# Gathers without a bound on the index: five stages of a graph network on one core

## The chip, the cores and the metric

The kernel runs on one core of a Trainium2 chip. The metric is the device time of one execution in microseconds (us). The kernel before took 9419.78 us, the median of three runs (9418.16 to 9432.5).

A core has five engines with queues of their own: TensorE (PE; its weight loads are PEld), VectorE (DVE), ScalarE (ACT), GpSimd (POOL) and SyncE (SP, which only issues transfers here). Sixteen DMA engines move the data. Gathers and scatters by a list of row numbers are issued on GpSimd.

## The reference

There are 100,000 nodes with 64 features each and 50,000 edges (`src`, `dst`), sorted by `dst`. Four layers follow one another, and each ends in a layer norm of the input plus the layer's output:

```python
def _tag_conv(x, row, col, norm, W, b):            # layer 0, twice, K = 5
    out = x @ W[0]
    h = x
    for k in range(1, K + 1):
        msg = h[row] * norm[:, None]
        h = jax.ops.segment_sum(msg, col, num_segments=N_NODES)
        out = out + h @ W[k]
    return out + b
# layer 1: mean over neighbours, then attention over edges and the node itself
agg = segment_sum(x[src], dst) / max(count, 1)
h = agg @ W_sl + b_sl + x @ W_sr
xl, xr = h @ Wg_l + bg_l, h @ Wg_r + bg_r           # 4 heads
logit = einsum('ehd,hd->eh', leaky_relu(xl[s2] + xr[d2], 0.2), att)
out = segment_sum(softmax(logit) * xl[s2], d2).mean(heads) + b_gat
# layer 2: relu(mean of (x @ W)[src] + x @ root + bias)
# layer 3: attention with logits a_src[src] + a_dst[dst], then a dense layer
```

Every `[src]` in it is a gather of rows, once for each of the 50,000 edges.

## The kernel before

The edges stand in 128 partitions of 391 columns each (`T = 391`, column T is padding), so one column is 128 edges, one in each partition. One gather fetches the source rows of one column: 128 rows of 64 to 68 floats from a table in device memory into a tile, by a list of 128 row numbers that stands in on-chip memory, one in each partition. Eight columns make a group (`K8 = 8`), 49 groups a stage (`NG`), and one stage has 391 gathers. The gathers of a stage go into a ring of six groups (`RING = 6`): before group g is gathered, GpSimd waits until group g - 6 has been consumed.

What happens in the order of time:

- The rows of x for all `dst` nodes are gathered (table `in_x_dram`), and beside it lie the dense layers of all nodes, computed as if no edge came in (the other nodes have rows of their own behind). They go on in slices beside most later stages of layer 0.
- First hop, kind "placed": rows of `x_with_place` (66 floats) by `src_index`. Every index is a node number below 100,000.
- Three more hops and the top stage gather by `place_of_source`: the row of the edge at which the source node's sum stands. A source without an edge into it has no such row; its index is set far outside of the table, the gather skips it by the bound, and what was in the tile before is multiplied by a weight of zero. Five more stages of the second convolution do the same with the tables y and u (nine stages by `place_of_source` in all, with 391 gathers each).
- Mean stage of layer 1 (table x1), by `row_of_source` (`comb`): a table that holds the 100,000 nodes followed by the rows of the edge places, 150,176 rows, so each index lies in it. VectorE sums the gathered columns (line 861), then TensorE, ScalarE and VectorE run 15 to 16 dependent steps for each group in three lanes.
- Pair stage of layer 1 (`logits2`, table `h_sage`), by `row_of_source`: TensorE turns the pairs of rows (line 2144) and computes the edge logits.
- The softmax terms and the attention sums of layer 1, without gathers apart from one.
- Mean stage of layer 2 (table x2), by `row_of_source`.
- Source rows of layer 3 (`logits3`, table x3), by `row_of_source`: VectorE adds the logits (line 2368), and SyncE writes the features back.
- Softmax terms and attention sums of layer 3, with a scatter of 392 columns into the output (line 2700), its index bounded as well.

All gathers go through one helper, `gather` (line 810, its instruction has line 812 in the profile), which gives each gather a bound and asks that an index over it be skipped in silence. `stage_gpsimd` (line 816) issues the gathers of the hops, of the up stages and of the two mean stages; the pair stage and the source rows have loops of their own. The order of the work is written out by hand: each engine has its own program, and waits are on semaphores.

Of the kernel before, what the change touches and what calls it, by code (L numbers as in the profile page):

```python
# [12 lines left out]
N = 100000  # L13
E = 50000
D = 64
# [8 lines left out]
RP = P * C  # L24
BLOCK = P * K8
DB = 98
CB = N
# [3 lines left out]
RING = 6  # L31
# [77 lines left out]
def bass_gnn_resnorm(nc, x, src, dst, edge_weight, edge_weight1, W0, b0, W1, b1, W_sl, b_sl, W_sr, Wg_l, bg_l,  # L109
# [21 lines left out]
    x66_rows = x66.rearrange("(n a) b -> n (a b)", a=XW // 2)  # L131
    xc = dram("xc", (RP, D))
    hop = [xc] + [dram(f"hop{k}", (RP, D)) for k in range(1, HOPS)]
# [4 lines left out]
    hh, x3 = (dram(n, (CB + RP, XL)) for n in ("h_sage", "x3"))  # L138
# [10 lines left out]
    srci = sb(stack, "src_index", [P, C], I32)  # L149
    comb = sb(stack, "row_of_source", [P, C], I32)  # L150
# [617 lines left out]
    norm, carried_b = PS[4][:, 0:C], PS[4][:, C:C + D]  # L768
# [40 lines left out]

    def gather(e, tab, index, into, top):  # L810

        return e.indirect_dma_start(out=into, out_offset=None, in_=tab,  # L812
                                    in_offset=bass.IndirectOffsetOnAxis(ap=index, axis=0), bounds_check=top,
                                    oob_is_err=False)

    def stage_gpsimd(e, st):
        top = e.to_reg(st.top)
        for g in range(NG):
            if g >= RING and st.weight is None:
                e.wait_ge(*st.summed((g - RING + 1) * K8))  # L820
            elif g >= RING:
                e.wait_ge(*st.weighed(g - RING + 1))
            for k in range(tiles(g)):
                t = g * K8 + k
                into = ring[g % RING][:, k, 0:XW if st.placed else D]
                gather(e, st.table, st.index[:, t:t + 1], into, top).then_inc(st.gathered[g % RING].handle, 16)
        if st.by_row:
            e.wait_ge(*st.headed(1))
            for i in range(3):
                e.wait_ge(*st.stored[i](16 * len(range(i, NG - 2, 3))))  # L830
            gather(e, st.into, early_row[:, 0:1], early_sum[0][:, :], RP - 1).then_inc(st.found_head.handle, 16)
# [216 lines left out]
    def main():  # L1048
        with ExitStack() as ctx:
# [72 lines left out]
            xs_out = [sem(f"x_out{i}", 16 * len(range(i, DB, 3))) for i in range(3)]  # L1122
            combined, lned = sem("combined", 4), sem("logarithm", NG)
            diag = sb(ctx, "first_dst", [P, P])
            hops = [Stage(x66_rows, N - 1, srci, norm, "placed", into=hop[1])]
            for k in range(2, HOPS):
                hops.append(Stage(hop[k - 1], RP - 1, found, norm, "hop", into=hop[k]))
            top = Stage(hop[HOPS - 1], RP - 1, found, norm, "top")
# [843 lines left out]
    def mean_stage(kind, tab, into, parts, own_part=None):  # L1972
        with ExitStack() as ctx:
            stage_buffers(ctx)
            st = Stage(tab, CB + RP - 1, comb, None, "mean")
            names = ("raw1", "raw2", "xT", "aT") + (("z0", "z1", "z2", "z3", "lin") if kind == "h" else ("a", "tmp"))
            lanes = [Work(ctx, f"lane{l}", MEAN_STEPS[kind], len(range(l, NG, MEAN_LANES)), [two], names, (1,), wide=(0,),
                          **(dict(full=OWN_ROUNDS, short=MEAN_SHORT) if kind == "h" else {}))
                     for l, two in enumerate(((PS[0], PS[1]), (PS[2], PS[3]), (PS[5], PS[6])))]
            for l, W in enumerate(lanes):  # L1980
                W.place = l

                def keep(r, _, l=l):
                    at = (MEAN_LANES * r + l) * K8
                    return parts[:, at:at + K8, :]

                def keep_own(r, _, l=l):
                    at = (MEAN_LANES * r + l) * K8
                    return own_part[:, at:at + K8, :]
                W.keep, W.keep_own = keep, keep_own  # L1990
            with nc.Block() as block:
                @block.gpsimd
                def _(e):
                    stage_gpsimd(e, st)

                @block.sync
                def _(e):
                    means_sync(e, lanes, kind, tab, into)

                @block.tensor  # L2000
                def _(e):
                    means_tensor(e, st, lanes, kind)

                @block.scalar
                def _(e):
                    mean_steps(lambda W: mean_scalar(e, W, kind), lanes).end()

                @block.vector
                def _(e):
                    means_vector(e, st, lanes, kind)  # L2010
# [67 lines left out]
    def logits2(parts, own_part, lg):  # L2078
        ORDER = list(range(NG))[::-1]
        PW = D + XL  # L2080
# [12 lines left out]
        got = [sem(f"row_gathered{i}", 16 * n) for i, n in enumerate([sum(tiles(g) for g in ORDER[i::RING]) for i in range(RING)])]  # L2093
# [6 lines left out]
        with ExitStack() as ctx:  # L2100
# [135 lines left out]
            with nc.Block() as block:  # L2236
# [28 lines left out]
                @block.gpsimd  # L2265
                def _(e):
                    e.wait_ge(*last_moved(1))
                    last_row = e.to_reg(CB + RP - 1)
                    for i in range(NG):
                        g = ORDER[i]  # L2270
                        if i >= RING:
                            e.wait_ge(*put[i % RING](16 * (i // RING)))
                            e.wait_ge(*taken(i - RING + 1))
                            e.wait_ge(*at(i - RING, 1))
                        for k in range(tiles(g)):
                            t = g * K8 + k
                            gather(e, hh, comb[:, t:t + 1], pair[i % RING][:, k, D:PW], last_row).then_inc(got[i % RING].handle, 16)

                @block.tensor
                def _(e):  # L2280
# [39 lines left out]
    def logits3(parts, lg):  # L2320
        fv, ft = sem("fill_vector", len(FILL)), sem("fill_tensor", 1)
        got = [sem(f"row_gathered{i}", 16 * n) for i, n in enumerate(in_slots(RING, tiles))]
        put = [sem(f"features_stored{i}", 16 * n) for i, n in enumerate(in_slots(RING, lambda g: 1))]
        met, done = sem("rows_met", NG), sem("logits_done", NG)
        with ExitStack() as ctx:
            rows_ = [sb(ctx, f"source_row{i}", [P, K8, XL]) for i in range(RING)]
            own = sb(ctx, "own_parts", [P, H2, C])
            fill = sb(ctx, "parts_of_node", [P, H2, C])
            last = sb(ctx, "parts_after", [P, H2])
            z = [sb(ctx, f"edge_logits{i}", [P, HEADS, K8]) for i in range(2)]  # L2330

            def got_all(g):
                return got[g % RING](16 * (K8 * (g // RING) + tiles(g)))

            with nc.Block() as block:
                @block.sync
                def _(e):
                    for g in range(NG):
                        e.wait_ge(*got_all(g))
                        e.dma_start(columns(hs_t, g)[:, 0:tiles(g), :], rows_[g % RING][:, 0:tiles(g), 0:D]  # L2340
                                    ).then_inc(put[g % RING].handle, 16)
                    for i in range(RING):
                        e.wait_ge(*put[i](16 * in_slots(RING, lambda g: 1)[i]))

                @block.gpsimd
                def _(e):
                    last_row = e.to_reg(CB + RP - 1)
                    for g in range(NG):
                        if g >= RING:
                            e.wait_ge(*put[g % RING](16 * (g // RING)))  # L2350
                            e.wait_ge(*met(g - RING + 1))
                        for k in range(tiles(g)):
                            t = g * K8 + k
                            gather(e, x3, comb[:, t:t + 1], rows_[g % RING][:, k, :], last_row).then_inc(got[g % RING].handle, 16)

                @block.tensor
                def _(e):
                    fill_tensor(e, fv, ft, own, PS[0])

                @block.vector  # L2360
                def _(e):
                    fill_vector(e, fv, ft, parts, own, fill, last, PS[0], lg)
                    for g in range(NG):
                        c, k = slice(g * K8, g * K8 + tiles(g)), tiles(g)
                        e.wait_ge(*got_all(g))
                        if g >= 2:
                            e.wait_ge(*done(g - 1))
                        e.tensor_tensor(z[g % 2][:, :, 0:k], rows_[g % RING][:, 0:k, D:XL].rearrange("p k h -> p h k"),
                                        own[:, 0:HEADS, c], ALU.add).then_inc(met.handle, 1)
                        e.wait_ge(*met(g + 1))  # L2370
                        e.scalar_tensor_tensor(lg[:, 0:HEADS, c], z[g % 2][:, :, 0:k], 0.2, z[g % 2][:, :, 0:k], ALU.mult,
                                               ALU.max).then_inc(done.handle, 1)
# [446 lines left out]
```

## Time and profile before

| what | value |
|---|---|
| median of the runs | 9419.78 us |
| span of the profiled execution | 9425.4 us |
| GpSimd busy | 6467.0 us, 69% of the span |
| TensorE busy | 5731.8 us, 61% |
| VectorE busy | 5330.6 us, 57% |
| ScalarE busy | 3226.1 us, 34% |
| gathers and scatters on GpSimd | 6264 instructions |
| bytes by GpSimd's DMA queue (q0) | 130.29 MB |

The profile is of one execution. Its span, from the first instruction to the last, is 5.6 us (0.06%) above the median of the runs, with next to nothing around it, so a difference worked out in the trace can be taken off either. Busy time of an engine is a sum over stages with different limits; a stage is judged by the engine that never waits in it.

### The profile page before, as it was taken

What the parts mean: (1) busy time and instruction counts of PE and PEld (TensorE: products, weight loads), DVE (VectorE), ACT (ScalarE), POOL (GpSimd) and SP (SyncE); (2) the same over time, 40 slices, a digit from 0 to 9 for tenths busy, and PEclk for the clock granted to TensorE, in tenths of its full rate; (3) what the DMA queues carried; (4) which work ended last, traced back from release to release, by engine and by line L of the source; (5) the groups of instructions that cost most, each with busy time, mean ns of one, the idle gap of its engine ahead of it and who ended that gap; (6) DMA issues with size and microseconds to landing.
All of it is one profiled execution on the core that took longest, in us unless ns stands there. A gap on an engine that the chain in (4) does not pass through costs nothing. (4 is left out here: it accounts for less than half of the span.)

```text
span 9425.4 us, 77459 instructions
## 1 busy us (share of the span) xinstructions
PE 5731.8 (61%) x19953; PEld 3098.8 (33%) x19953; DVE 5330.6 (57%) x14589; ACT 3226.1 (34%) x5537; POOL 6467.0 (69%) x6274
## 2 busy tenths in 40 slices
PE   6656565665669865564646200598997976610397
PEld 5623232333335422232323100243334644300264
DVE  4235454554546566666656588544458965510596
ACT  0034343443423333343424101243445753300153
POOL 7777777777777577777777777775770017767477
PEclk7578787887879977787778655799998988855698
DMA  6764332332369733232323222222334532222353
GB/s 164 127 141 120 99 104 86 103 103 86 103 173 261 224 94 99 89 100 84 104 85 99 80 76 81 66 72 70 80 76 139 188 125 75 73 48 52 91 178 119
DMA packets 1086302, 1021.92 MB, mean 108 GB/s; under 512 B 653551, under 2 KB 709245, under 8 KB 1073313
## 3 DMA queue, kind: packets, MB, share of 16 engines
q1 hardware_dynamic: 847422, 884.62, 30.3%
q0 software_dynamic: 200480, 130.29, 7.8%
q10 hardware_dynamic: 37955, 2.05, 0.4%
q8 instruction: 160, 2.62, 0.1%
q14 instruction: 285, 2.33, 0.1%
HBM read 494.44 MB, written 599.31 MB: 116 GB/s over the span
## 5 line engine op out<-in xcount | busy, mean ns | idle before, releaser
L812 POOL DMA_INDIRECT gathered<-u,place_of_source x1564 | 1641.3, 1049 | 512.9 <-issue 475.3
L812 POOL DMA_INDIRECT gathered<-hop,place_of_source x1564 | 1608.0, 1028 | 508.5 <-issue 475.3
L847 DVE TENSOR_TENSOR weighted<-gathered,bank 128x512 f32<-128x512 f32 (+1 forms) x490 | 335.7, 685 | 1408.6 <-DMA gathered<-hop,place_of_source 688.0
L861 DVE SCALAR_TENSOR_TENSOR sums<-sums,same_as_before,weighted 128x64 f32<-128x64 f32 x3510 | 987.2, 281 | 96.3 <-DVE weighted L847 40.8
L812 POOL DMA_INDIRECT gathered<-x,row_of_source x782 | 806.5, 1031 | 298.3 <-issue 234.6
L874 DVE SCALAR_TENSOR_TENSOR first_node_sum<-sums,ends_first,first_node_sum 128x64 f32<-128x64 f32 x2786 | 782.2, 281 | 7.1 <-DVE sums L861 5.9
L531 PE MATMUL bank<-dense_tmp,mean 128*128 128x512 f32 x980 | 527.1, 654 | 77.7 <-ACT dense_tmp L540 76.2
L2700 POOL DMA_INDIRECT out_dram<-lane_out,node_to_write x392 | 396.0, 1010 | 215.6 <-issue 116.1
L812 POOL DMA_INDIRECT gathered<-y,place_of_source x391 | 408.1, 1044 | 187.5 <-issue 118.8
L835 PE MATMUL bank<-sums,goes_on_into 128*128 128x64 f32 x22 | 7.6, 448 | 857.7 <-DVE sums L861 857.7
L812 POOL DMA_INDIRECT pair<-h_sage,row_of_source x391 | 406.6, 1040 | 171.7 <-issue 117.3
L531 PE MATMUL bank<-dense_a,center 128*128 128x512 f32 x588 | 416.7, 823 | 163.4 <-DVE dense_a L555 109.8
L812 POOL DMA_INDIRECT source_row<-x,row_of_source x391 | 397.7, 1017 | 153.9 <-issue 118.8
L812 POOL DMA_INDIRECT gathered<-x_with_place,src_index x391 | 400.3, 1024 | 138.1 <-issue 137.8
L812 POOL DMA_INDIRECT gathered<-in_x_dram,dst_index x392 | 394.2, 1006 | 135.5 <-issue 117.9
L531 PE MATMUL bank<-dense_yT,bd_l 128*128 128x512 f32 x196 | 184.5, 1041 | 473.6 <-DVE dense_out L516 473.4
L812 POOL DMA_INDIRECT first_sum<-head_sums,row_of_first_end x2 | 2.0, 1025 | 616.1 <-DMA head_sums<-head_sums 615.8
L2742 DVE SCALAR_TENSOR_TENSOR head_sums<-head_sums,same_as_before 128x256 f32<-128x256 f32 x780 | 380.1, 487 | 24.5
L2563 PE MATMUL bank<-ident,heads 128*128 128x128 f32 x1568 | 361.8, 278 | 41.0 <-issue 18.5
L861 DVE SCALAR_TENSOR_TENSOR sums<-sums,same_as_before,gathered 128x64 f32<-128x64 f32 x780 | 218.2, 280 | 269.1 <-DMA gathered<-x,row_of_source 269.0
L2564 PE MATMUL bank<-ident,head_sums 128*128 128x128 f32 x1568 | 357.6, 275 | 0.0
L542 ACT ACTIVATE dense_tmp<-bank,eps_col 128x512 f32<-128x512 f32 x490 | 332.3, 678 | 52.2 <-PE bank L531 51.6
(533 smaller groups left out, 14427.4 us busy)
## 6 DMA issues: line engine op xcount, KB each, us to landing
head_sums<-head_sums SPq DMA_DIRECT2D x98, 1024.0 KB, 4.7
y<-conv_out SPq DMA_DIRECT2D x294, 256.0 KB
conv_out<-y SPq DMA_DIRECT2D x245, 256.0 KB, 3.2
hop<-sums SPq DMA_DIRECT2D x196, 256.0 KB, 2.0
turned<-rows_turned SPq DMA_DIRECT2D x196, 256.0 KB, 2.7
cat<-turned SPq DMA_DIRECT2D x196, 256.0 KB
u<-conv_out SPq DMA_DIRECT2D x196, 256.0 KB, 2.0
lane_raw<-x SPq DMA_DIRECT2D x196, 256.0 KB
```

What stands on the lines that cost most here:

```text
L531: m = e.matmul(W.bank[l][b][:, :], w, W.b(v, l), start=i == 0, stop=i == len(pairs) - 1)
L542: m = e.activation(W.b(o, l), src_ap, func, bias=v[:, 0:1], scale=scale)
L812: return e.indirect_dma_start(out=into, out_offset=None, in_=tab, in_offset=bass.IndirectOffsetOnAxis(ap=index, axis=0), bounds_check=top, ...
L835: e.matmul(carried_b, link[:], s[:, K8 - 2, :], start=True, stop=True).then_inc(st.carried.handle, 1)
L847: e.tensor_tensor(weighted[g % 2][:, 0:n, :], st.rows_of(g), over(st.weight[:, cols], D), ALU.mult).then_inc(st.weighed.handle, 1)
L861: e.scalar_tensor_tensor(s[:, k, :], b, go[:, t:t + 1], m[:, k, :], ALU.mult, ALU.add).then_inc(st.summed.handle, 1)
L874: e.scalar_tensor_tensor(h, row_, flast[:, t:t + 1], h, ALU.mult, ALU.add).then_inc(st.headed.handle, 1)
L2563: e.matmul(to, o[:, at_], ident[:], start=True, stop=False, is_transpose=True)
L2564: m = e.matmul(to, s[:, at_], ident[:], start=False, stop=True, is_transpose=True)
L2700: e.indirect_dma_start(out=out, out_offset=bass.IndirectOffsetOnAxis(ap=scat[:, t:t + 1], axis=0), in_=W.out[0][0][:, k * D:(k + 1) * D], ...
L2742: e.scalar_tensor_tensor(s[:, k, :], b, go[:, t:t + 1], s[:, k, :], ALU.mult, ALU.add).then_inc(summed.handle, 1)
```

## The change

A gather may now be called with no bound (`top` is None). Five stages do so: the first hop, the mean stages of layers 1 and 2, the pair stage and the source rows, with 391 gathers each. The other gathers and the scatter keep the bound and the silent skip. In the call without a bound, `oob_is_err=False` is left out as well. No instruction changes its place on any engine; five register moves on GpSimd go, one for each of the five stages, since no register is loaded with the bound.

```diff
     def gather(e, tab, index, into, top):
 
-        return e.indirect_dma_start(out=into, out_offset=None, in_=tab,
-                                    in_offset=bass.IndirectOffsetOnAxis(ap=index, axis=0), bounds_check=top,
-                                    oob_is_err=False)
+        at = bass.IndirectOffsetOnAxis(ap=index, axis=0)
+        if top is None:
+            return e.indirect_dma_start(out=into, out_offset=None, in_=tab, in_offset=at)
+        return e.indirect_dma_start(out=into, out_offset=None, in_=tab, in_offset=at, bounds_check=top, oob_is_err=False)
 
     def stage_gpsimd(e, st):
-        top = e.to_reg(st.top)
+        top = None if st.top is None else e.to_reg(st.top)
...
-            hops = [Stage(x66_rows, N - 1, srci, norm, "placed", into=hop[1])]
+            hops = [Stage(x66_rows, None, srci, norm, "placed", into=hop[1])]
...
-            st = Stage(tab, CB + RP - 1, comb, None, "mean")
+            st = Stage(tab, None, comb, None, "mean")
...
-                    last_row = e.to_reg(CB + RP - 1)
...
-                            gather(e, hh, comb[:, t:t + 1], pair[i % RING][:, k, D:PW], last_row).then_inc(got[i % RING].handle, 16)
+                            gather(e, hh, comb[:, t:t + 1], pair[i % RING][:, k, D:PW], None).then_inc(got[i % RING].handle, 16)
...
-                    last_row = e.to_reg(CB + RP - 1)
...
-                            gather(e, x3, comb[:, t:t + 1], rows_[g % RING][:, k, :], last_row).then_inc(got[g % RING].handle, 16)
+                            gather(e, x3, comb[:, t:t + 1], rows_[g % RING][:, k, :], None).then_inc(got[g % RING].handle, 16)
```

## Rows read from the trace of the kernel before

**Rows 1.** The profile's page, part 1: busy us of each engine.
```profile
PE 5731.8 (61%) x19953; PEld 3098.8 (33%) x19953; DVE 5330.6 (57%) x14589; ACT 3226.1 (34%) x5537; POOL 6467.0 (69%) x6274
```

**Rows 2.** Groups on GpSimd: count, busy us, mean ns of one, idle before.
```profile
L812 POOL DMA_INDIRECT gathered<-x,row_of_source x782 | 806.5, 1031 | 298.3 <-issue 234.6 <-POOLq L2636 37.8 <-POOLq L1534 18.4
...
L812 POOL DMA_INDIRECT source_row<-x,row_of_source x391 | 397.7, 1017 | 153.9 <-issue 118.8 <-ACTq L2335 35.0
...
L1540 POOL IOTA sums<- 128x496 int32 x1 | 0.5, 540 | 0.0
L1538 POOL IOTA conv_out<- 128x392 int32 x1 | 0.5, 453 | 6.5 <-DVE same_as_next L1789 6.5
...
L288 POOL TENSOR_SCALAR_AFFINE_SELECT ident<-ident 128x128 f32<-128x128 f32 x1 | 0.3, 292 | 4.1 <-DVE eps_col L334 4.1
```

**Rows 3.** GpSimd in order of time, source rows: start us, duration us, idle before.
```profile
8400.04 0.99 POOL L812 DMA_INDIRECT source_row<-x,row_of_source  x1 [0.30 <-issue]
8401.34 0.99 POOL L812 DMA_INDIRECT source_row<-x,row_of_source  x1 [0.30 <-issue]
```

**Rows 4.** Busy us by stage: first hop, mean 1, pair, mean 2, source rows.
```profile
562.00:1081.20 519.20, 321.25 (x1013) 168.01 (x1011) 272.00 (x741) 224.76 (x383) 400.31 (x391) 0.79 0.39 113
...
5971.20:6488.30 517.10, 491.06 (x1652) 202.85 (x1652) 212.50 (x944) 201.00 (x331) 393.71 (x391) 0.96 0.27 70
6541.10:7066.50 525.40, 471.25 (x1498) 173.80 (x1498) 266.60 (x1007) 229.23 (x375) 406.55 (x391) 0.96 0.38 78
7721.10:8252.70 531.60, 346.59 (x1102) 203.24 (x1102) 279.41 (x1082) 168.04 (x276) 412.74 (x391) 0.79 0.29 72
8287.70:8804.20 516.50, 0.60 (x2) 0.50 (x2) 41.44 (x119) 0.00 (x0) 397.69 (x391) 0.50 0.26 51
```

**Rows 5.** Line 812 in the source rows: duration min/median/max ns, and who waited.
```profile
L812 POOL DMA_INDIRECT source_row<-x,row_of_source x391: 992/997/3142, 8287.7 to 8803.2; - x196
...
  DVE edge_logits L2368: 474.8, 48
```

**Rows 6.** Waits of 562 to 1090, first hop: us in total, times, longest.
```profile
DVE bank L843 <- DMA gathered<-x_with_place,src_index: 179.8, 46, 7.7
```

**Rows 7.** Waits of 7721 to 8290, mean stage of layer 2.
```profile
DVE sums L861 <- DMA gathered<-x,row_of_source: 241.2, 48, 6.8
```

**Rows 8.** Waits of 6541 to 7080, pair stage.
```profile
PEld bank L2144 <- DMA pair<-h_sage,row_of_source: 48.2, 21, 4.4
...
PE bank L2144 <- DMA pair<-h_sage,row_of_source: 29.0, 14, 3.4
```

**Rows 9.** Mean stage of layer 1, busy us within 100 us, as in group 4.
```profile
6300.00:6400.00 100.00, 100.00 (x339) 40.35 (x337) 43.33 (x191) 40.65 (x68) 76.55 (x78) 1.00 0.28 74
```

**Rows 10.** Line 861 in the mean stage of layer 1: duration ns, first and last.
```profile
L861 DVE SCALAR_TENSOR_TENSOR sums<-sums,same_as_before,gathered x390: 270/279/327, 5983.1 to 6520.2; 128x64 f32<-128x64 f32 x195
```

**Rows 11.** Line 812 in the same stage: duration ns, first and last start us.
```profile
L812 POOL DMA_INDIRECT gathered<-x,row_of_source x391: 992/997/1399, 5971.2 to 6487.3; - x196
...
  DVE sums L861: 7.5, 10
```

**Rows 12.** GpSimd in order of time, mean stage of layer 1, ring full.
```profile
6430.02 0.99 POOL L812 DMA_INDIRECT gathered<-x,row_of_source  x1 [0.30 <-issue]
6432.00 1.39 POOL L812 DMA_INDIRECT gathered<-x,row_of_source  x1 [0.99 <-DVE sums L861]
```

**Rows 13.** Line 812 in a hop by place of source: duration min/median/max ns.
```profile
L812 POOL DMA_INDIRECT gathered<-hop,place_of_source x391: 991/997/1608, 1090.3 to 1610.5; - x196
L812 POOLq MOVE  x1: 29/29/29, 1599.1 to 1599.1; - x1
```

**Rows 14.** GpSimd's DMA queue, 1100 to 1600, that hop: packets, MB, share.
```profile
q0 software_dynamic: 11984, 4.45, 5.6%
```

**Rows 15.** GpSimd's DMA queue, 8300 to 8800, source rows.
```profile
q0 software_dynamic: 12223, 13.32, 15.9%
```

**Rows 16.** The scatter into the output, line 2700: duration min/median/max ns.
```profile
L2700 POOL DMA_INDIRECT out_dram<-lane_out,node_to_write x392: 980/982/1238, 8899.0 to 9416.2; - x196
```

## The prediction, made before the result was known

> **What bounds the kernel now.** I read the busy times first, then the groups on GpSimd, then each stage for itself. No engine is busy all the time [rows 1], but GpSimd's 69% understates it: between two gathers of a stage it stands for 0.30 us with nothing to wait for [rows 3], time that the page calls issue. The typical gather takes 0.997 us [rows 5], so one column costs 1.30 us, and 391 of them about 509 us. The five stages that the change touches last 517 to 532 us from the first gather to the end of the last [rows 4]. Four of them are therefore one unbroken train of gathers.
>
> Who waits for whom says the same. In the first hop VectorE stood 179.8 us, 46 times, for the gathers of a group [rows 6], in the mean stage of layer 2 241.2 us [rows 7], and in the source rows 474.8 us, where TensorE and ScalarE do nothing at all [rows 4, 5]. In the pair stage TensorE is busy 471 of 525 us, and its queue still stood 48.2 us for gathered rows at the weight loads and 29.0 us at the matmuls [rows 8]: GpSimd sets the pace, with little in hand.
>
> The mean stage of layer 1 is the odd one. TensorE is busy for 100.00 of 100 us at a granted clock of 1.00, the upper of its two levels, 2.4 GHz [rows 9]. The gathers start from 5971.2 to 6487.3, but the sums that consume them from 5983.1 to 6520.2 [rows 10, 11]: 12 us behind at the start, 33 us at the end. From 6432.0 on the ring of six groups is full, and GpSimd waits for VectorE's sums [rows 12], ten waits of 7.5 us in all [rows 11]. That stage ends when TensorE is through, not when the gathers are.
>
> **The change part by part.** Nothing is added and nothing moves. It removes the bound from 5 x 391 = 1955 gathers, and five register moves of 29 ns on GpSimd [rows 13], 0.15 us in all, which I leave out. The count of gathers, their sizes, the ring and all waits stay. The whole effect is then one number, the ns that a gather takes less (or more) without its bound, times the gathers that stand on the path.
>
> The path: the first hop, the pair stage, the mean stage of layer 2 and the source rows count in full, 4 x 391 = 1564 gathers. The mean stage of layer 1 counts nothing as long as the saving is small: a faster GpSimd only fills the ring earlier and then waits longer for the sums. The work that covers its 391 gathers is TensorE's, 491 us of the 517 [rows 4]. Were TensorE no cover, a saving of s ns would be worth 0.391 s us more.
>
> What one bound costs the trace of before doesn't show, since every gather in it has one. The nearest rows bound it:
>
> - What the check decides costs no time. In a hop by place of source GpSimd's queue moved 4.45 MB in 11,984 packets within 500 us, in the source rows 13.32 MB in 12,223 [rows 14, 15]. At 1.30 us a gather that is 32 packets each, while the bytes fall from 272 for each row to about 92 (256 without a skip): most rows of the hop are skipped, and each leaves its entry behind. Yet both have the same typical duration, 997 ns, and the same fastest, 991 and 992 [rows 5, 13]. So there is no branch for a skipped row that would make the gather shorter; if the check costs time, it is the same for every index.
> - Upper end: a compare and select over 128 indices one after another. IOTA takes 453 ns for 392 columns and 540 for 496 [rows 2], so 0.84 ns a column after a start of about 125. An AFFINE_SELECT, which compares and selects, over 128 columns takes 292 ns, 167 above that start [rows 2].
> - Lower end: the indices stand one in each partition, so one column of such a compare might do for all: 167 / 128 = 1.3 ns.
> - The nearest row is that of another form of the same instruction. The scatter has as many indices, also bounded, on the other side of the transfer, and takes 982 ns instead of 997 [rows 16, 5], 15 ns less. That is how much these forms differ, and it bounds the other sign as well: without the bound a gather might also take 15 ns more.
>
> I take 15 ns, the one difference measured between two forms of this instruction, and nearer to the lower end than to the upper. The sum: 1564 x 15 = 23.5 us. Against the profiled span it is 9425.4 - 23.5 = 9401.9; that span lies 5.6 us above the median, so the time forecast is 9419.8 - 23.5 = 9396.3.
>
> A rule speaks against the change. The rows show 32 packets for each gather with and without skipped rows, and one typical duration [rows 5, 13 to 15]. The Trainium skill, page "DMA: Bandwidth & Descriptors", section "SWDGE vs HWDGE vs iDMA", says that a transfer issued on GpSimd has its descriptors computed by software, one pair for each operation, and written into rings. If that writing were the whole of the 997 ns, the change would take nothing off, since the number of entries is set by the 128 indices: the time would be 9419.8. The trace agrees that the entries stay; no row shows what part of the 997 ns they are.
>
> **The rivals.**
>
> - The bound costs nothing: it is one operation among many for all indices, or the instruction compares with some bound in any case, and the lower end of 1.3 ns holds. For it: the duration that doesn't move with the share of skipped rows. Against it: skipped rows are given another size, so something is selected for each row, and forms of the instruction do differ by 15 ns. 1564 x 1.3 = 2 us, 9418.
> - The bound costs much, 40 ns or more, as in a loop over the indices. For it: 997 ns for 128 indices is 7.8 ns for each, the length of a loop rather than of one operation for all. Against it: nothing but the missing evidence. Then the pair stage stops giving when TensorE no longer waits for rows, at most 48.2 us, which is reached at 123 ns a gather; and the mean stage of layer 1 still gives nothing. At 80 ns: 4 x 391 x 80 = 125 us, if TensorE's waits in the pair stage all go, 9295. At the upper end, 167 ns: 3 x 391 x 167 + 48.2 = 244 us, 9176.
> - Slower. The new call drops `oob_is_err=False` together with the bound, so by its argument an index out of the table is now an error and no longer skipped. If this form tests each index and reports instead of selecting a size, a gather takes longer, and by the 15 ns between two forms it is 1564 x 15 = 23.5 us, 9443. It decides from 12 ns a gather (0.2% of the time). For it: the argument in the diff. Against it: without a bound there is nothing to test against except the table's own size, which the call doesn't name. The mean stage of layer 1 would hide it too.
> - TensorE is no cover in the mean stage of layer 1. That adds 0.391 x 15 = 5.9 us of gain, 9390; the full ring speaks against it.
>
> **How the numbers follow.** A difference under 0.2%, 19 us, can't be told from no change by a measurement of this kernel; over 1564 gathers that is 12 ns each. The forecast, a saving of 6 to 40 ns, has 39% (its own range is 9357 to 9410), 8 of them below 12 ns; the last rival shares these. No cost, under 6 ns in either direction, 30%. Much, 40 ns and more, 17%. Longer by over 6 ns, 14%, 2 of them within 12 ns. So faster is 31 + 17 = 48%, no change 8 + 30 + 2 = 40%, slower 12%. The range reaches up to 13 ns longer, 9440, and down to 100 ns saved: 3 x 391 x 100 + 39 = 156 us, 9264, rounded to 9265. What is left out below is the rest of the way to 9176, some 8%, above some 7%.
>
> **What would show it.** Line by line in the profile after: the gathers without a bound by their minimum and median (997 before), the gathers that keep it and the scatter, which must stay at 997 and 982; the idle 0.30 us before each gather, where the cost could stand instead of in the duration; the five stages' lengths, of which the mean stage of layer 1 should keep its end while its ring is full earlier and the waits for the sums grow from 7.5 us (by some 5.9); and the queue's 32 packets a gather. I am wrong if the unbounded gathers differ by nothing (then 9418), if they take longer, or if the stages don't shorten by 391 times what one gather saves.

## The result and the profile after

The changed kernel takes 9338.08 us, the median of four runs (9333.71 to 9342.84), against 9422.83 us for the kernel before beside it: 84.8 us less, a ratio of 0.9911 with a 95% interval of 0.9899 to 0.9923. The forecast was 9396 us within 9265 to 9440.

The groups on GpSimd tell most of it (count, busy us, mean ns of one, idle before). Line 814 is now the gather without a bound, line 815 the one that keeps it, and line 2699 the scatter.

```profile
L815 POOL DMA_INDIRECT gathered<-hop,place_of_source x1564 | 1606.6, 1027 | 506.9 <-issue 475.4 <-DMA hop<-sums 31.5
L814 POOL DMA_INDIRECT gathered<-x,row_of_source x782 | 765.2, 978 | 305.9 <-issue 232.3 <-POOLq L2635 38.0 <-DVE sums L862 18.0
...
L814 POOL DMA_INDIRECT source_row<-x,row_of_source x391 | 377.9, 967 | 153.5 <-issue 118.8 <-ACTq L2335 34.7
```

The means fall by 50 ns in the source rows (from 1017 in [rows 2]) and by 53 ns in the two mean stages together (from 1031). The 53 there is an average of two unlike numbers: by the busy times of [rows 4] and of the table below, the mean falls by 26 ns in layer 1 (1007 to 981) and by 80 in layer 2 (1056 to 976). Minimum, median and maximum of one instruction show the step without the disturbed ones; here are line 814 in the source rows with its waiter, line 815 in the hop of [rows 13], and the scatter:

```profile
L814 POOL DMA_INDIRECT source_row<-x,row_of_source x391: 940/944/3146, 8213.6 to 8709.4; - x196
...
  DVE edge_logits L2367: 454.7, 48
```
```profile
L815 POOL DMA_INDIRECT gathered<-hop,place_of_source x391: 992/997/1600, 1070.8 to 1589.1; - x196
```
```profile
L2699 POOL DMA_INDIRECT out_dram<-lane_out,node_to_write x392: 982/982/1251, 8805.5 to 9322.8; - x196
```

Without its bound a gather takes 944 ns where it took 997 [rows 5]; the idle before it is the same (118.8 us over 390 gathers, 0.305 us each), and the forms that keep the bound stay at 997 and 982. So s, the one unknown of the prediction, is 53 ns.

Busy us by stage (columns as in [rows 4]: length, then PE, PEld, DVE, ACT and POOL, granted clock, DMA share, GB/s):

```profile
562.10:1061.70 499.60, 313.12 (x1014) 163.81 (x1012) 272.49 (x741) 224.81 (x383) 380.73 (x391) 0.82 0.40 117
5943.90:6458.80 514.90, 489.82 (x1648) 201.94 (x1649) 211.41 (x944) 200.41 (x330) 383.55 (x391) 0.96 0.26 71
6511.50:7023.70 512.20, 468.04 (x1498) 171.87 (x1498) 266.56 (x1007) 228.80 (x375) 393.28 (x391) 0.97 0.38 80
7678.40:8178.90 500.50, 335.34 (x1098) 192.32 (x1099) 279.45 (x1082) 166.82 (x276) 381.59 (x391) 0.81 0.29 76
8213.60:8710.30 496.70, 0.60 (x2) 0.50 (x2) 41.69 (x119) 0.00 (x0) 377.86 (x391) 0.50 0.26 53
```

From the first gather of a stage to the first one of the next (for the source rows: to the first scatter), the first hop lasts 508.7 us instead of 528.3, the mean stage of layer 1 567.6 instead of 569.9, the pair stage with what follows it 1166.9 instead of 1180.0, the mean stage of layer 2 535.2 instead of 566.6, and the source rows with the softmax terms 591.9 instead of 611.3. That is 19.6, 2.3, 13.1, 31.4 and 19.4 us, 85.8 together. The spans of the two profiled executions differ by 93.4 us (9425.4 and 9332.0); the other 7.6 us lie in stages that the change doesn't touch. (All these are differences of one profiled execution each.)

The mean stage of layer 1 does what the prediction said. Line 862, the sums, with its waiters, and TensorE within 50 us:

```profile
L862 DVE SCALAR_TENSOR_TENSOR sums<-sums,same_as_before,gathered x390: 266/277/325, 5955.3 to 6491.2; 128x64 f32<-128x64 f32 x195
...
  POOL gathered L814: 18.0, 18
```
```profile
6300.00:6350.00 50.00, 50.00 (x170) 20.27 (x168) 21.08 (x95) 20.72 (x34) 38.00 (x40) 1.00 0.26 70
```

The sums run over 535.9 us instead of 537.1 [rows 10], though the gathers are 53 ns shorter; GpSimd waits for them 18 times, 18.0 us, instead of 7.5 [rows 11]. Its gathers there are busy for 383.6 us instead of 393.7, so the 10 us that they gave up came back as waiting.

### The profile page after: what moved, and what is told of

Read it like the earlier page. It is cut to its first block and busy times, and to the rows that moved or that the text cites. A ratio compares the mean times of both kernels' runs of the same rounds, so it can differ in the third digit from the quotient of the medians.

```text
span 9332.0 us, 77454 instructions
## 1 busy us (share of the span) xinstructions
PE 5706.7 (61%) x19953; PEld 3078.5 (33%) x19953; DVE 5329.1 (57%) x14589; ACT 3223.6 (35%) x5537; POOL 6368.2 (68%) x6274
## 5 line engine op out<-in xcount | busy, mean ns | idle before, releaser
L814 POOL DMA_INDIRECT gathered<-x,row_of_source x782 | 765.2, 978 | 305.9 <-issue 232.3
L2699 POOL DMA_INDIRECT out_dram<-lane_out,node_to_write x392 | 395.8, 1010 | 216.2 <-issue 116.4
L815 POOL DMA_INDIRECT gathered<-y,place_of_source x391 | 405.8, 1038 | 187.0 <-issue 118.8
L814 POOL DMA_INDIRECT pair<-h_sage,row_of_source x391 | 393.3, 1006 | 171.6 <-issue 113.7
L815 POOL DMA_INDIRECT gathered<-in_x_dram,dst_index x392 | 394.4, 1006 | 135.7 <-issue 118.2
L814 POOL DMA_INDIRECT source_row<-x,row_of_source x391 | 377.9, 967 | 153.5 <-issue 118.8
L814 POOL DMA_INDIRECT gathered<-x_with_place,src_index x391 | 380.7, 974 | 137.8 <-issue 137.8
```

What stands on the lines that cost most here:

```text
L2699: e.indirect_dma_start(out=out, out_offset=bass.IndirectOffsetOnAxis(ap=scat[:, t:t + 1], axis=0), in_=W.out[0][0][:, k * D:(k + 1) * D], ...
```

## The experiments

**The changed kernel again, and the bound put back stage by stage.** Four kernels on one chip. One is the changed kernel again, the mark for the others; in the other three one stage has its bound again: the mean stage of layer 1, the pair stage, and the mean stage of layer 2.

```diff
-            st = Stage(tab, None, comb, None, "mean")
+            st = Stage(tab, CB + RP - 1 if kind == "h" else None, comb, None, "mean")
```
```diff
...
-                            gather(e, hh, comb[:, t:t + 1], pair[i % RING][:, k, D:PW], None).then_inc(got[i % RING].handle, 16)
+                            gather(e, hh, comb[:, t:t + 1], pair[i % RING][:, k, D:PW], last_row).then_inc(got[i % RING].handle, 16)
...
```
```diff
-            st = Stage(tab, None, comb, None, "mean")
+            st = Stage(tab, CB + RP - 1 if kind == "x3" else None, comb, None, "mean")
```

The mark, without any bound put back:

> The changed kernel again, as the mark for the three others of this call. If the gain is the sum of its stages as the two traces have it (first hop 19.5, mean stage of layer 1 2.3, pair stage 13.1, mean stage of layer 2 31.4, source rows 19.4 us, together 85.7), it is 80 to 92 us below the kernel before on this chip too, and its profile has unbounded gathers of 944 ns median. If the 31.4 us of the mean stage of layer 2 were the luck of one profiled execution, its mean of a gather there (976 ns) lies 20 ns or more away from that.

It took 9337.26 us, ratio 0.9913 [0.9899, 0.9926], so 84.3 us below the kernel before here. But in its mean stage of layer 2 a gather takes 1004 ns on average, not 976, as the groups within the stage show, first of the changed kernel's first profile, then of this one:

```profile
L814 POOL DMA_INDIRECT gathered<-x,row_of_source x391 | 381.6, 976 | 156.9 <-issue 118.9 <-POOLq L2635 38.0
```
```profile
L814 POOL DMA_INDIRECT gathered<-x,row_of_source x391 | 392.6, 1004 | 154.2 <-issue 118.8 <-POOLq L2635 35.4
```

That is 28 ns away, so part of the 31.4 us there was the luck of one execution. The bound in the mean stage of layer 1:

> The changed kernel with the bound put back in the mean stage of layer 1 alone. Theory (TensorE ends that stage, the bound there is hidden): 0 to 5 us above the changed kernel; its gathers are 997 ns again, the stage from its first gather to the first gather of the pair stage is 570 us instead of 567.6. Rival (gathers count there as everywhere): 391 x 53 ns = 20.7 us above.

9335.79 us, ratio 0.9909 [0.9893, 0.9924]: 1.5 us below the mark, no difference. GpSimd's group in that stage, with its wait for the sums, of this kernel:

```profile
L815 POOL DMA_INDIRECT gathered<-x,row_of_source x391 | 394.2, 1008 | 140.7 <-issue 113.6 <-POOLq L1535 17.7 <-DVE sums L862 9.4
```

The 391 gathers are 53 ns longer at the median (997 again) and 27 ns at the mean (1008 against 981), which puts 10.6 us back on GpSimd; its wait for the sums shrinks to 9.4 us, and nothing ends later. That these gathers are not on the path is shown, not only argued; that TensorE is what covers them rests on its busy share. The pair stage:

> The changed kernel with the bound put back in the pair stage alone. Theory (the faster gathers lose 8 of their 20.7 us to work of VectorE that they now meet): 11 to 16 us above the changed kernel, mean of a gather about 1040 ns against 1006. Rival (each gather counts in full): 20.7 us above. Second rival (TensorE takes over): under 8 us, and TensorE waits no longer for gathered rows in the changed kernel.

9350.92 us, ratio 0.9931 [0.9917, 0.9945]: 13.7 us above the mark. First this kernel's group, then that of the changed kernel's first profile:

```profile
L815 POOL DMA_INDIRECT pair<-h_sage,row_of_source x391 | 405.7, 1038 | 171.8 <-issue 117.0 <-DVE pair L2297 53.0 <-ACT quad_z L2183 1.5
```
```profile
L814 POOL DMA_INDIRECT pair<-h_sage,row_of_source x391 | 393.3, 1006 | 171.6 <-issue 113.7 <-DVE pair L2296 52.7 <-ACT quad_z L2183 2.1
```

32 ns for each of 391 gathers are 12.5 us: the time follows the mean of a gather, and the median's 53 ns don't arrive in full. TensorE hasn't taken over, since it still waits for gathered rows, 37.9 us at the weight loads (48.2 before, [rows 8]). The mean stage of layer 2:

> The changed kernel with the bound put back in the mean stage of layer 2 alone. Theory (20.7 us by the bound, and some 11 us because the sixth gather of a group no longer meets VectorE's multiply of 128x512): 27 to 35 us above the changed kernel, mean of a gather about 1056 ns against 976. Rival (the 11 us are chance): 18 to 23 us above, mean of a gather under 1035 ns.

9363.77 us, ratio 0.994 [0.9927, 0.9954]: 26.5 us above the mark, between what the two expected. Its gathers there:

```profile
L815 POOL DMA_INDIRECT gathered<-x,row_of_source x391 | 411.5, 1053 | 157.5 <-issue 118.8 <-POOLq L2635 38.7
```

1053 ns, where the profile of before has 1056, while the four profiles so far without the bound there (the changed kernel's two and those of the two kernels just told of) show 976, 1004, 989 and 992, 990 on average. 63 x 391 ns are 24.6 us: 20.7 by the bound and some 4 because, on the average of the four, fewer gathers are held up, so 7 of the 31.4 us were chance. The columns differ, too: of the 23 us that the gathers of this stage exceed their median by in the profile of before, 19 fall on the sixth of each group of eight, the one that VectorE's multiply of 128x512 mostly overlaps. What that overlap does is read further down.

**Which part of the bound costs.** One kernel gathers the source rows, where the other engines are nearly idle, in all forms side by side:

```diff
+                            if k in (0, 3, 6):
+                                e.indirect_dma_start(out=r[:, k, :], out_offset=None, in_=x3, in_offset=at(t)).then_inc(s_, 16)
+                            elif k in (1, 4, 7):
+                                e.indirect_dma_start(out=r[:, k, :], out_offset=None, in_=x3, in_offset=at(t), bounds_check=last_row, oob_is_err=False).then_inc(s_, 16)
+                            else:
+                                e.indirect_dma_start(out=r[:, k, :], out_offset=None, in_=x3, in_offset=at(t), bounds_check=last_row, oob_is_err=True).then_inc(s_, 16)
+                            if k == 3:
+                                e.indirect_dma_start(out=h[0:N2, 0, :], out_offset=None, in_=x3, in_offset=at(t, N2)).then_inc(s_, 16)
+                            if k == 4:
+                                e.indirect_dma_start(out=h[0:N2, 1, :], out_offset=None, in_=x3, in_offset=at(t, N2), bounds_check=last_row, oob_is_err=False).then_inc(s_, 16)
...
```

> The changed kernel, whose source-row stage (VectorE and TensorE nearly idle) gathers its columns in three forms in turn: without a bound, with the bound and the silent skip, with the bound and an index over it as an error; and for two columns of each group 64 of the 128 rows once more into a spare tile, without and with the bound. Theory (the test against the bound costs): 944, 997 and 997 ns. Rival (the silent skip costs): 944, 997 and 944 ns. A cost for each index halves with 64 rows: 26 ns between the two halves; a cost for each instruction stays 53 ns. If the whole gather is a loop over its indices, 64 rows take some 500 ns; if it is fixed, over 800.

Minimum, median and maximum ns, in the order of the diff: no bound (line 2359), silent skip (2361), error (2363), 64 rows without (2365) and with a bound (2367):

```profile
L2359 POOL DMA_INDIRECT source_row<-x,row_of_source x147: 953/957/3083, 8220.7 to 8855.5; - x147
...
L2361 POOL DMA_INDIRECT source_row<-x,row_of_source x146: 992/997/2640, 8222.7 to 8851.6; - x146
...
L2363 POOL DMA_INDIRECT source_row<-x,row_of_source x98: 1012/1024/1767, 8225.6 to 8854.2; - x98
...
L2365 POOL DMA_INDIRECT half_row<-x,row_of_source x49: 905/909/921, 8230.9 to 8850.4; - x49
...
L2367 POOL DMA_INDIRECT half_row<-x,row_of_source x49: 947/951/1244, 8233.8 to 8852.9; - x49
```

(Its one run, 9480.47 us, holds 98 gathers more than the changed kernel.) The silent skip isn't what costs: with an error instead of the skip the gather is longest. It is the bound in either form; whether comparing with it or fetching it costs, no run separates. Its price doesn't halve with the rows: it is 42 ns with 64 rows (951 - 909), and 40 with 128 in this kernel (997 - 957), 53 in stages of one form. So of the two rivals on its shape a price for each instruction is nearer. And 64 rows take 909 ns, only 35 to 48 less than 128 (944 or 957), so the gather is almost wholly a cost of the instruction. Its packets don't halve either. The changed kernel's queue over the whole span, then this kernel's with its 98 gathers of 64 rows:

```profile
q0 software_dynamic: 200480, 130.29, 7.4%
```
```profile
q0 software_dynamic: 203616, 132.00, 7.1%
```

The 3136 packets more are 32 for each of the 98, as for 128 rows.

One thing is confounded here: in this mixture a gather without a bound takes 957 instead of 944. It isn't simply the form of the gather before it, since in the kernel with two forms in turn (below) those that follow one of their like at the border of two groups take 957, too, at the median of 24 in either mean stage. The cause stays open. A kernel with one form alone settles the order:

```diff
...
-                                    oob_is_err=False)
+                                    oob_is_err=err)
...
-                gather(e, st.table, st.index[:, t:t + 1], into, top).then_inc(st.gathered[g % RING].handle, 16)
+                gather(e, st.table, st.index[:, t:t + 1], into, top, st.kind in ("placed", "mean")).then_inc(st.gathered[g % RING].handle, 16)
...
```

> The kernel before, whose gathers in the five stages keep the bound but name an index over it an error (no index is). Theory (the test costs): the time of the kernel before within 8 us, 997 ns. Rival (the silent skip costs): the changed kernel's time, some 84 us below, 944 ns. Third (the error form costs extra): above the kernel before.

```profile
L812 POOL DMA_INDIRECT source_row<-x,row_of_source x391: 1006/1010/3141, 8291.9 to 8812.6; - x196
```

9439.06 us, ratio 1.0025 [1.0015, 1.0035]: slower than the kernel before, by some 23 us on this chip (9416.35 there). The third expectation held. 1564 x 13 ns are 20.3 us.

**Are gathers without a bound held up more?** The excess over the median in the pair stage grew with the change (1040 - 997 = 43 ns before; 1006 - 945 = 61 in the changed kernel's first profile, 50 in its second), so both forms were set side by side there and in the mean stages:

```diff
...
-                            gather(e, hh, comb[:, t:t + 1], pair[i % RING][:, k, D:PW], None).then_inc(got[i % RING].handle, 16)
+                            gather(e, hh, comb[:, t:t + 1], pair[i % RING][:, k, D:PW], row_ if (k + i) % 2 else None).then_inc(got[i % RING].handle, 16)
```

> The changed kernel, whose gathers in the two mean stages and in the pair stage have the bound or not in turn, column by column, so both forms meet the same work of VectorE. The excess of a gather's mean over its median in the pair stage was 43 ns with the bound and 50 to 62 without. If the form without a bound is held up more by VectorE, its excess in the pair stage is again 10 ns or more above the other's; if the changed pace decides when they meet, the two forms have the same excess within 6 ns. Time between the changed kernel's and the one before.

```profile
L815 POOL DMA_INDIRECT pair<-h_sage,row_of_source x195 | 204.0, 1046 | 59.5 <-issue 57.3 <-ACT quad_z L2184 1.5 <-PE bank L2140 0.3
L814 POOL DMA_INDIRECT pair<-h_sage,row_of_source x196 | 193.2, 986 | 111.1 <-issue 59.1 <-DVE pair L2298 51.7 <-PE bank L2146 0.3
```

Minimum, median and maximum there, with the bound and without:

```profile
L815 POOL DMA_INDIRECT pair<-h_sage,row_of_source x195: 992/1006/2665, 6513.2 to 7027.0; - x195
```
```profile
L814 POOL DMA_INDIRECT pair<-h_sage,row_of_source x196: 940/956/3281, 6512.0 to 7025.7; - x196
```

The excess over the form's own median is 40 ns with the bound and 30 without (49 and 42 over the 997 and 944 of stages of one form). So in the same stretch the form without a bound is held up no more, rather less, and by more than the 6 ns that the expectation allowed for "the same". It isn't the form that makes the excess grow; that the faster pace does is what remains, not shown by a run of its own. The time, one run, was 9363.51 us, between the two kernels.

What holds up a gather in the mean stages can be read in the traces. VectorE multiplies each group of sums in one instruction (128x512, line 1042 before, 1043 after). Here are start and duration in us, first before, where a gather starts while the multiply runs, then after, where the multiply starts within a gather:

```profile
7976.38 0.69 DVE L1042 TENSOR_TENSOR lane_raw<-sums,one_over_count 128x512 f32<-128x512 f32 x1
```
```profile
7976.46 1.48 POOL L812 DMA_INDIRECT gathered<-x,row_of_source  x1 [0.30 <-issue]
```
```profile
7919.10 0.94 POOL L814 DMA_INDIRECT gathered<-x,row_of_source  x1 [0.30 <-issue]
```
```profile
7919.28 0.68 DVE L1043 TENSOR_TENSOR lane_raw<-sums,one_over_count 128x512 f32<-128x512 f32 x1
```

In the mean stage of layer 2 before, 42 gathers take over 100 ns more than the median. All 42 start while the multiply runs, and each is longer by what was left of it less 0.12 to 0.13 us; the six multiplies that start within a gather don't make it over 100 ns longer. After, 34 multiplies start within a gather and 14 catch one at its start. So the chance in this stage is the point of the train at which the multiply falls. In the mean stage of layer 1 it went the other way, 6 gathers over 100 ns longer before and 30 after, all beside the multiply, which is why the mean fell by 26 ns there. In the pair stage the like multiply (line 2220 before, 2221 after) accounts in the same way for 7.6 of an excess of 16.7 us before and for 10.1 of 23.8 after; what makes up the rest was not settled.

**The bound off everywhere.** In the nine stages by place of source most indices lie outside on purpose. Two kernels send those sources to a row inside the table, where their weight of zero makes the row harmless:

```diff
-            e.tensor_copy(found[:, cols], ring[g % RING][:, 0:n, 0].bitcast(I32))
+            e.tensor_scalar(found[:, cols], ring[g % RING][:, 0:n, 0].bitcast(I32), RP - 1, None, ALU.min)
...
-                hops.append(Stage(hop[k - 1], RP - 1, found, norm, "hop", into=hop[k]))
+                hops.append(Stage(hop[k - 1], None, found, norm, "hop", into=hop[k]))
...
```

> The changed kernel, whose nine stages by place of source have no bound either: a source without a row is sent to the table's last row (its weight is zero) by a minimum in place of a copy. Theory (a gather is worth 53 ns wherever GpSimd is the bound): 9 x 391 x 53 ns = 187 us below the changed kernel, about 9150 us, less what VectorE and TensorE take over. Rival (the rows that were skipped now move, three times the bytes and most of them from one row of the table): GpSimd's gathers are 944 ns, but they land late and VectorE waits; 0 to 60 us below, or above.

9465.71 us, ratio 1.0044 [1.0028, 1.0061]: slower than the kernel before, and 128 us slower than the changed one (the mark). GpSimd's queue in the hop of [rows 14] (1100 to 1600 us), GpSimd's largest new wait, and the top stage, all of this kernel:

```profile
q0 software_dynamic: 11830, 12.15, 67.4%
```
```profile
POOL gathered L814 <- DVE weighted L848: 232.9, 50, 20.6
```
```profile
2668.60:3337.40 668.80, 519.67 (x1493) 268.70 (x1494) 307.71 (x976) 172.03 (x331) 378.26 (x391) 0.88 0.98 196
```

The gathers are short (944 ns), but their packets take 67.4% of the DMA engines' time instead of 5.6%, and the top stage lasts 669 us, 526 in the changed kernel (2654.7 to 3180.4). Two causes fit: nearly three times the bytes (12.15 MB against 4.45), or one row read by most of the packets. The last kernel changes only which row is read, by adding each absent source's own edge row less the mark for absent:

```diff
...
+            e.scalar_tensor_tensor(shift[:, g % 2, 0:n], place, float(ABSENT), own_less[:, cols], ALU.is_ge, ALU.mult)
...
+            e.tensor_tensor(found[:, cols], place, shift[:, g % 2, 0:n], ALU.add)
...
```

> As the kernel with all sources inside the table, but a source without a row is sent to the row of its own edge (128 different rows in each gather) instead of the table's last row for all. Theory (it was the one hot row that slowed the transfers there, 67.4% of the DMA engines' time for 12.15 MB): the transfers of GpSimd's queue in a hop fall to some 13% of the engines' time, as in the source rows, GpSimd waits no longer for weighted groups, and the nine stages give up to 187 us: 9150 to 9190 us. Rival (it was the bytes, three times as many): over 9400 us again.

9167.21 us, ratio 0.9724 [0.9711, 0.9738]. The same queue row (1100 to 1560 us), and line 816, its gather without a bound, in that hop:

```profile
q0 software_dynamic: 11488, 11.79, 13.6%
```
```profile
L816 POOL DMA_INDIRECT gathered<-hop,place_of_source x391: 938/944/1475, 1075.0 to 1574.1; - x196
```

As many bytes a gather cost 13.6% when spread: the hot row was the cause. This kernel is 258 us below the one before on its chip (9425.63), and so some 174 us better than the changed kernel's 84, of the 187 that nine stages of 391 gathers at 53 ns would give. It is the fastest of all here.

## Why the prediction was right, and where its size was off

**What bounds the kernel: right.** Four of the five stages are a train of gathers on GpSimd. VectorE still waits 454.7 us for the source rows (474.8 in [rows 5]), and the time per stage follows the mean of a gather.

**The mean stage of layer 1 counts nothing: right.** Putting the bound back there, 10.6 us of GpSimd time, changed the time by -1.5 us, within the uncertainty. The waits for the sums grew by 10.5 us instead of the 5.9 foreseen, because the saving was larger, 10 us of busy time.

**The term that was mis-sized: the 15 ns.** The step that was off is "I take 15 ns, the one difference measured between two forms of this instruction". Measured it is 53. With it the same sum gives 1564 x 53 = 82.9 us, and 84.8 came: the saving is 3.6 times the 23.5 us of the forecast, and the time lies in the range only because that was kept wide, down to 100 ns a gather. The scatter's 15 ns is the price of another difference; scatter and gather both have a bound, so its price isn't in it. The end of 167 ns, from a compare and select, bounded the truth, and the constant 997 ns with and without skipped rows did say that the bound's price, if there is one, doesn't hang on what the check decides; it didn't say that it is small. The 53 ns lie in the case that had 17%, 40 ns and more, whose picture was wrong as well: it took the gather for a loop over 128 indices, but half the rows take only 35 to 48 ns off.

**The rule weighed against the change.** The Trainium skill, page "DMA: Bandwidth & Descriptors", section "SWDGE vs HWDGE vs iDMA", has one pair of descriptors computed for each operation. The trace agrees that the queue's packets stayed (12147 in 480 us of the source rows, 32 a gather), and yet the gather became 53 ns shorter: the bound's price was not hidden behind the entries. What part of the remaining 944 ns they are stays open, because a gather of 64 rows leaves 32 packets, too.

**The rival of the other sign** named a real mechanism, that the form with an error costs more than the silent skip: 13 ns, 1010 against 997, which made a kernel slower by 0.25%. It doesn't apply to the changed kernel: without a bound the gather is the shortest of all forms, with the argument left out.

**Stage by stage** two of the four counted stages stand clearly apart from 20.7 us: the pair stage gives 13 to 14, the mean stage of layer 2 25 to 27 in the runs with its bound put back. Gathers held up, mostly those that start while VectorE's multiply runs, move the mean of that stage by up to 28 ns from one execution to the next (976 and 1004) at the same median of 944. The prediction had no term for that. That the sum with 53 ns comes so near to 84.8 is therefore partly luck: the pair stage gave some 7 us less than 20.7, the mean stage of layer 2 some 6 us more.

## What to carry to other kernels

When one engine issues a long unbroken train of like instructions, a few per cent of one instruction are that share of every stage it bounds; count the stages where another engine sets the end apart, by who waits at a full ring. A bound on gathered indices is paid on every gather, so leave it off where the indices can be proved, or made, to lie inside; but spread the made ones over different rows, since one hot row cost more than all the bounds together. Where no row shows the price of the thing removed, a neighbour's difference is no estimate: keep the whole interval between the bounds. And a stage's saving is count times the mean, not the median: look which gathers start beside the other engine's long instruction, before and after.

## What was not expected of the hardware

- A gather on GpSimd costs 944 ns for 128 rows (957 where forms are mixed) and 909 for 64, with 32 packets either way, so it is nearly a fixed price for each instruction.
- The bound costs 53 ns with a silent skip and 66 with an error for an index over it.
- A mixture of forms costs, too: a gather without a bound takes 957 ns at the median there, 944 in a stage of its like. Why is open.
- A gather that starts while VectorE's multiply of 128x512 (0.68 us) runs is longer by what is left of it less 0.12 to 0.13 us, up to some 0.5 us; one that had started before it in the mean stage of layer 2 kept its length, in 33 of 34 cases after the change.
- Most packets of a gather reading one and the same row took 67.4% of the DMA engines' time for 12.15 MB in 500 us; 11.79 MB from different rows in 460 us took 13.6%.
